# Down product of an expert slot: the last 48 inner rows as two split float32r passes instead of one fp32 product

## The reference

```python
E, K, I, SI = (16, 4, 176, 704)
topk_w, topk_idx = jax.lax.top_k(routing_probs, K)      # 4 of 16 experts per token
shared = _silu_mul(x @ shared_gate_up.T, SI) @ shared_down.T
def step(acc, ew):
    w_gu, w_d, cw = ew
    h = _silu_mul(x @ w_gu.T, I)                        # silu(gate) * up, 176 inner rows
    return (acc + h @ w_d.T * cw[:, None], None)
```

## Time and profile before

| | before |
|---|---|
| median of 3 runs | 1028.64 us (1028.04 to 1030.07) |
| profiled execution, device time | 1030.14 us |
| its span, first to last instruction | 1028.1 us |
| TensorE busy | 962.3 us (94%) |
| VectorE busy | 825.4 us (80%) |
| ScalarE busy | 379.4 us (37%) |
| GpSimd busy | 509.6 us (50%) |
| mean granted TensorE clock | 0.975 |

### The profile page before, as it was taken

How to read it: one execution, slowest core, us unless ns; L and a number is a source line. 1 busy time by engine, 2 the same in 40 slices (tenths; PEclk the granted TensorE clock), 3 DMA queues, 4 the chain that set the end, 5 groups by cost and what they waited for, 6 DMA issues and landing times.

```text
span 1028.1 us, 17347 instructions
## 1 busy us (share of the span) xinstructions
PE 962.3 (94%) x5569; PEld 853.8 (83%) x5569; DVE 825.4 (80%) x1583; ACT 379.4 (37%) x1063; POOL 509.6 (50%) x384
## 2 busy tenths in 40 slices
PE   4799799999999898999999999979899999999997
PEld 4688689888988897888888898867788799999986
DVE  4989989999989999878989988865677766666647
ACT  2454443542333443322345222242154244444430
POOL 0525335366534436575624557614633366666660
PEclk9899999999999999999999999998999999999999
DMA  9789669997347412102521220225151277777769
GB/s 350 281 310 391 260 249 353 408 361 246 144 149 253 187 64 83 62 32 94 207 81 62 83 84 22 75 82 219 53 196 43 80 117 121 120 118 122 118 94 311
DMA packets 67192, 171.84 MB, mean 167 GB/s; under 512 B 6561, under 2 KB 40097, under 8 KB 65953
## 3 DMA queue, kind: packets, MB, share of 16 engines
q1 hardware_dynamic: 52656, 151.69, 40.3%
q0 software_dynamic: 14448, 19.05, 11.3%
HBM read 84.72 MB, written 85.99 MB: 166 GB/s over the span
## 4 chain that ended last, share of the span: by engine, by line
PE 64%; DVE 24%; issue 5%; DMA 3%; POOL 2%; ACT 1%; SPq 0%; DVEq 0%; ACTq 0%; POOLq 0%
PE bank L477 8%; PE bank L479 8%; PE bank L478 8%; DVE rot L1350 5%; PE bank L557 5%; PE bank L687 4%; DVE rot L1347 4%; PE bank L710 4%; PE bank L831 3%; PE bank L833 3%; DVE turn L1334 2%; PE bank L580 2%; PE bank L792 2%; PE bank L582 2%; PE bank L581 2%
## 5 line engine op out<-in xcount | busy, mean ns | idle before, releaser
L1160 POOL TENSOR_TENSOR rot<-turn 64x512 f32<-64x512 f32 x64 | 91.5, 1430 | 260.2 <-DVE turn L1334 234.2
L1334 DVE SCALAR_TENSOR_TENSOR turn<-bank,bqk,trig 128x1024 f32<-128x1024 f32 x128 | 160.7, 1276 | 14.1 <-PE bank L479 12.0
L1228 POOL DMA_INDIRECT sums<-ysb,token_at x79 | 123.0, 1557 | 70.2 <-DMA sums<-ysb,token_at 29.6
L477 PE MATMUL bank<-xt_hi,w_hi 128*128 128x512 f32 x256 | 106.7, 417 | 15.1 <-DVE turn L1334 9.8
L1193 POOL TENSOR_TENSOR kv<-c_t,v_t 128x512 f32<-128x512 f32 x64 | 69.2, 1095 | 98.4 <-ACT v_t L960 46.0
L687 PE MATMUL bank<-wo,z_t 128*128 128x256 f32 x512 | 116.0, 379 | 0.8 <-ACT z_t L1031 0.8
L687 PEld LDWEIGHTS bank<-wo,z_t 128*128 128x128 f32 x512 | 94.9, 190 | 12.8 <-ACT z_t L1031 1.0
L992 ACT ACTIVATE prob<-prob,negmax 128x128 f32<-128x128 f32 x256 | 98.9, 390 | 6.9 <-DVE negmax L1319 6.7
L479 PE MATMUL bank<-xt_hi,w_lo 128*128 128x512 f32 x256 | 100.5, 393 | 0.0
L478 PE MATMUL bank<-xt_lo,w_hi 128*128 128x512 f32 x256 | 100.4, 392 | 0.0
L1002 ACT COPY v<-bank 128x512 f32<-128x512 f32 x64 | 37.5, 586 | 164.2 <-PE bank L479 164.2
(11 more groups left out here) (183 smaller groups left out, 2417.9 us busy)
## 6 DMA issues: line engine op xcount, KB each, us to landing
xs<-zeros SPq DMA_DIRECT2D x12, 3710.0 KB, 16.8
w_hi<-w_dram SPq DMA_DIRECT2D x24, 768.0 KB, 4.4
w_lo<-w_dram SPq DMA_DIRECT2D x24, 768.0 KB, 7.0
xe_all<-xs SPq DMA_DIRECT2D x79, 132.5 KB, 2.6
sums<-zeros SPq DMA_DIRECT2D x3, 2176.0 KB, 12.8
raw<-in_wqkv SPq DMA_DIRECT2D x16, 384.0 KB, 4.3
w_dram<-w_hi SPq DMA_DIRECT2D x8, 768.0 KB, 5.7
w_dram<-w_lo SPq DMA_DIRECT2D x8, 768.0 KB, 7.0
```

The costliest lines, as they stand in the source:

```text
L477: nc.tensor.matmul(o, lh, rh, start=(i == 0), stop=False)
L1228: nc.gpsimd.indirect_dma_start(sums_dram[s % SUMS], bass.IndirectOffsetOnAxis(ap=token_at[:, s:s + 1], axis=0), ysb[s % YBUFS][:], None, c ...
L1334: last = nc.vector.scalar_tensor_tensor(turn_all[m][:, 2 * i:2 * i + 2, :], qk_bank[2 * m + i][:].unsqueeze(1).to_broadcast([128, 2, GT]), ...
```

## The change

The inner rows 128 to 175 no longer go through an fp32 product. `slot_mult` writes them twice into `eh`, at columns 128 to 175 and 192 to 239 (the second by an instruction of its own), so that after the transpose they stand on partitions 0 to 47 and again on 64 to 111. ScalarE takes the turned half as float32r into `rest_hi`; VectorE writes the low part of the upper copy into `rest_lo`, whose lower half is zero. The down weights of these rows, `dnp`, hold their low part on partitions 0 to 63 and their high part on 64 to 127. One pass `rest_hi` x `dnp` then gives high x low plus high x high, and one pass `rest_lo` x `dnp` gives low x high. The low and high parts of `dnp` are made in four parts during the third shared group: ScalarE rounds (two copies of 64x1024, the lower one into the buffer `again`), VectorE subtracts, each waiting for the other. ScalarE's gate goes to a buffer of its own (`sg`) and no longer into `eh`. YBUFS goes from 4 to 3, for room.

```diff
-YBUFS = 4
+YBUFS = 3
...
+PARTS_DOWN = EXPERTS // GB
...
-        eht = [sb(f"eht{i}", [128, 2, 128], c=gctx) for i in range(2)]
+        eht = [sb(f"eht{i}", [128, 128], c=gctx) for i in range(2)]
+        rest_hi = [sb(f"rest_hi{i}", [128, 128], F32R, gctx) for i in range(2)]
+        rest_lo = [sb(f"rest_lo{i}", [128, 128], F32R, gctx) for i in range(2)]
...
-            for part in range(2):
-                e = slice(part * EXPERTS // 2, (part + 1) * EXPERTS // 2)
-                sp.dma_start(dne[:, e], down_in[:, e]).then_inc(down_loaded, 16)
+            sp.dma_start(dnp[:].bitcast(F32), down2_in).then_inc(down_loaded, 16)
+            sp.dma_start(dne[:], down_in).then_inc(down_loaded, 16)
...
                 if s >= 2:
                     pe.wait_ge(eht_taken, s - 1)
+                    pe.wait_ge(rest_lo_done, s - 1)
...
-                nc.tensor.matmul(o, eht[s % 2][:, 0, :], dne[:, e, 0, :].rearrange("p a n -> p (a n)"),
-                                 start=True, stop=False)
-                nc.tensor.matmul(o, eht[s % 2][:, 1, :], dne[:, e, 1, :].rearrange("p a n -> p (a n)"),
-                                 start=False, stop=True).then_inc(ey_ready, 1)
+                w1 = dne[:, e, :].rearrange("p a n -> p (a n)")
+                w2 = dnp[:, e, :].rearrange("p a n -> p (a n)")
+                nc.tensor.matmul(o, eht[s % 2][:], w1, start=True, stop=False)
+                pe.wait_ge(rest_hi_done, s + 1)
+                nc.tensor.matmul(o, rest_hi[s % 2][:], w2, start=False, stop=False)
+                pe.wait_ge(rest_lo_done, s + 1)
+                nc.tensor.matmul(o, rest_lo[s % 2][:], w2, start=False, stop=True).then_inc(ey_ready, 1)
...
+            def rest_high(part):
+                e = slice(part * GB, (part + 1) * GB)
+                if part == 0:
+                    act.wait_ge(down_loaded, 3 * 16)
+                    act.wait_ge(tt_ready, CH * len(TURNS))
+                act.wait_ge(dnp_lo_done, part)
+                nc.scalar.copy(again[0:64].bitcast(F32R), dnp[0:64, e].bitcast(F32))
+                nc.scalar.copy(dnp[64:128, e], dnp[64:128, e].bitcast(F32)).then_inc(dnp_hi_done, 1)
+
             for i in range(SCH):
                 shared_silu(2, i)
+                if i < PARTS_DOWN:
+                    rest_high(i)
+            act.wait_ge(dnp_lo_done, PARTS_DOWN)
...
-                if s >= 2:
-                    act.wait_ge(eht_ready, s - 1)
-                nc.scalar.activation(eh[s % 2][:, 0:INTER], banks[2 + s % 2][:, 0:INTER], ACT.Silu).then_inc(es_done, 1)
+                if s < 2:
+                    act.wait_ge(hm_done, 3 * SCH)
+                else:
+                    act.wait_ge(eh_done, s - 1)
+                nc.scalar.activation(sg[(s + 1) % 2][:, 0:INTER], banks[2 + s % 2][:, 0:INTER], ACT.Silu).then_inc(es_done, 1)
...
-                nc.scalar.copy(eht[s % 2][:], banks[4 + s % 2][:, 0:256].rearrange("p (c t) -> p c t", c=2)).then_inc(eht_taken, 1)
+                nc.scalar.copy(rest_hi[s % 2][:], banks[4 + s % 2][:, 128:256]).then_inc(rest_hi_done, 1)
+                nc.scalar.copy(eht[s % 2][:], banks[4 + s % 2][:, 0:128]).then_inc(eht_taken, 1)
...
+            def rest_low(part):
+                e = slice(part * GB, (part + 1) * GB)
+                dve.wait_ge(dnp_hi_done, part + 1)
+                nc.vector.tensor_tensor(dnp[0:64, e], dnp[0:64, e].bitcast(F32), again[0:64], ALU.subtract).then_inc(dnp_lo_done, 1)
...
+                if i < PARTS_DOWN:
+                    rest_low(i)
...
-                h = eh[s % 2][:, 0:INTER]
-                nc.vector.tensor_tensor(h, banks[2 + s % 2][:, INTER:2 * INTER], h, ALU.mult).then_inc(eh_done, 1)
+                if s >= 2:
+                    dve.wait_ge(eht_ready, s - 1)
+                h, up = sg[(s + 1) % 2][:, 0:INTER], banks[2 + s % 2][:, INTER:2 * INTER]
+                nc.vector.tensor_tensor(eh[s % 2][:, 0:INTER], up, h, ALU.mult)
+                nc.vector.tensor_tensor(eh[s % 2][:, 192:192 + IREST], up[:, 128:INTER], h[:, 128:INTER], ALU.mult).then_inc(eh_done, 1)
...
+            def slot_rest(s):
+                dve.wait_ge(eht_taken, s + 1)
+                if s >= 2:
+                    dve.wait_ge(ey_ready, s - 1)
+                nc.vector.tensor_tensor(rest_lo[s % 2][64:128, :], banks[4 + s % 2][64:128, 128:256],
+                                        rest_hi[s % 2][64:128, :].bitcast(F32), ALU.subtract).then_inc(rest_lo_done, 1)
...
                 if s >= 2:
                     slot_out(s - 2)
+                if 1 <= s <= SLOTS:
+                    slot_rest(s - 1)
```

More of the change, by code:

```diff
@@ L68, in decoder @@
 def decoder(nc, x_in, wqkv_in, bqk_in, bv_in, wo_in, bo_in, trig_in, mask_in, ident_in,
-            ctx_in, ctxt_in, skip_in, toep_in, same_in, gate_in, gue_in, gus_in, down_in, downs_in,
+            ctx_in, ctxt_in, skip_in, toep_in, same_in, gate_in, gue_in, gus_in, down_in, down2_in, downs_in,
             count_in, route_in, out):
@@ L224, in decoder @@
         gue_hi = sb("gue_hi", [128, EXPERTS, CH, 2 * INTER], F32R, ectx)
-        dne = sb("dne", [128, EXPERTS, 2, D], c=ectx)
+        dne = sb("dne", [128, EXPERTS, D], c=ectx)
+        dnp = sb("dnp", [128, EXPERTS, D], F32R, ectx)
         ectx.close()
@@ L331, in decoder @@
         eht_taken = sem("eht_taken")
+        rest_hi_done = sem("rest_hi_done")
+        rest_lo_done = sem("rest_lo_done")
+        dnp_hi_done = sem("dnp_hi_done")
+        dnp_lo_done = sem("dnp_lo_done")
         ey_ready = sem("ey_ready")
@@ L758, in shared_up @@
                     pe.wait_ge(eht_taken, SLOTS - 1)
+                    pe.wait_ge(rest_lo_done, SLOTS - 1)
                     shared_block(SCH - 1 + i, banks[4 + at], q).then_inc(upb_ready, 1)
@@ L775, in shared_up @@
                     pe.wait_ge(eht_taken, SLOTS)
+                    pe.wait_ge(rest_lo_done, SLOTS)
                 if i < SCH - 1 and ups:
@@ L912, in _ @@
             pe.wait_ge(down_loaded, 3 * 16)
+            pe.wait_ge(dnp_hi_done, PARTS_DOWN)
+            pe.wait_ge(dnp_lo_done, PARTS_DOWN)
             experts = [slot_expert(0), None, None, None]
@@ L1718, in _ @@
             for i in range(2):
-                nc.vector.memset(eh[i][:, INTER:256], 0.0)
+                nc.vector.memset(eh[i][:, INTER:192], 0.0)
+                nc.vector.memset(eh[i][:, 192 + IREST:256], 0.0)
+                nc.vector.memset(rest_lo[i][0:64, :].bitcast(F32), 0.0)
             shared_add(2)
@@ L1750 @@
 _INS = ["x", "wqkv", "bqk", "bv", "wo", "bo", "trig", "mask", "ident", "ctx", "ctxt", "skip", "toep", "same", "gate",
-        "gue", "gus", "down", "downs", "count", "route"]
+        "gue", "gus", "down", "down2", "downs", "count", "route"]
 def layouts(x, fside_S2_0, ctx_2048, L0_attn_W_Q, L0_attn_b_Q, L0_attn_W_K, L0_attn_b_K, L0_attn_W_V, L0_attn_b_V,
@@ L1771, in layouts @@
     dwn = a(L0_ffn_expert_down).transpose(2, 0, 1)
-    down = np.zeros((128, EXPERTS, 2, D), np.float32)
-    down[:, :, 0], down[:IREST, :, 1] = dwn[:128], dwn[128:]
+    down2 = np.zeros((128, EXPERTS, D), np.float32)
+    down2[:IREST], down2[64:64 + IREST] = dwn[128:], dwn[128:]
     sdn = a(L0_ffn_shared_down).T
@@ L1801, in layouts @@
         "gus": gus.reshape(SBLK * 128, CH, 128).transpose(2, 1, 0),
-        "down": down,
+        "down": dwn[:128],
+        "down2": down2,
         "downs": downs,
```

## The result

The changed kernel took 1023.97 us (median of 5 runs, 1022.51 to 1024.83), the kernel before, on the same chip, 1030.07 (5 runs, 1028.04 to 1031.82). The ratio is 0.994, 95% interval 0.9921 to 0.9958: a gain of 6.1 us where 15 were forecast, and 1024 lies outside the range of 1011.5 to 1021.5. The profiled execution has a span of 1022.0 us at 1023.97; the span of before was 1028.1, 6.1 more.

The account below looks back on a forecast made before the run. TensorE was taken to bound the slot stage. The profiled 1030.14 us, less 15.1 in the slots, plus 0.3 ahead of them, gave 1015.3, and 1013.8 as median; the 8-in-10 range was 1011.5 to 1021.5.

Parts of the forecast that it names:

- TensorE per slot: Slot stage: two 0.12 us passes replace a 0.434 us fp32 product, period 2.26 to 2.07, saving 0.194 us per slot.
- the 15.1: Forecast TensorE gain over the slots in us: 0.194 x 78, slot 77 left out.
- The ring: Three output buffers in the slots: costs nothing or a few tenths once; rival that it binds, 1035 us, chance 0.03.
- VectorE per slot: Slot stage: two added instructions of 0.14 and 0.29 us stay hidden; idle falls from 0.65 to 0.16 us per slot.
- The thinnest cover: Slots: VectorE's low part is ready 0.25 us before the last pass's weight load; each 0.1 above costs up to 7.9 us.
- ScalarE per slot: Slot stage: one 0.37 us copy becomes two of 0.27, ending 0.07 us later, hidden with 0.4 to spare.
- Before the slots: Splitting the packed down weights ahead of the slots: ScalarE copies and VectorE subtractions cost 0.3 us, bounds 0 and 1.5.
- The first slot transpose should stand at 813.4 as now: Sign in the profile after: TensorE's first transpose of slot rows starts at 813.4 us, unmoved.
- The forecast's last 1.5: Step from the profiled execution's 1015.3 us to the median forecast of 1013.8, as before's profiled execution was 1.5 above its median.
- a cover of 1.64 us: TensorE's 1.64 us idle before the first slot transpose, waiting for a DMA, was to cover the late second block.
- the 1.1 of the prediction: Ahead of the slots: VectorE's L1525 of the second block comes 1.1 us late, and TensorE with it.

Follow-up runs that it names:

- the four buffers: Changed kernel with a fourth ysb buffer (YBUFS = 4) in an idle half of hs; 1021.44 us, ratio 0.9838 to the kernel before.
- the first filler: Changed kernel plus twelve 128x256 products on TensorE ahead of the first slot transpose; 1020.83 us, ratio 0.9844 to the kernel before.
- rows in PSUM: Changed kernel with rounded lower rows in PSUM, a fourth output buffer and twelve products ahead of the first slot transpose; 1020.34 us, ratio 0.9891.
- the padded one: Kernel before plus forty more long-met waits on ScalarE, at about 750 us; 1032.18 us, ratio 1.0017.

## Why the prediction was wrong

- **TensorE per slot: right.** Passes 0.12, period 2.26 to 2.07. Over the 78 periods from first to last turn the medians, 2.260 and 2.073, give 14.6 of the 15.1. The step to 12.9 is slots over the usual period: 2.7 us of them after, 1.0 before. After, two of them (2.42 and 2.29) stand at the full ring and some ten, of 2.1 to 2.3, are scattered. The ring explains 0.3 to 0.6; the others are not settled.
- **VectorE per slot: right.** 0.12 and 0.29 for the forecast 0.14 and 0.29, idle 0.21 for 0.16. The thinnest cover held but for one wait of 0.3.
- **ScalarE per slot: right.** 0.27 each.
- **The ring: right**, a few tenths.
- **Before the slots: wrong, and most of the miss.** The term was "I take 0.3 us in all; bounds are 0 and 1.5", and the sign "The first slot transpose should stand at 813.4 as now". It was 7.0, and the transpose stood at 818.32. From the forecast of 1015.3 for the profiled execution to its 1023.97 there are 8.7 us: 6.7 are this term, 2.2 the slots, -0.2 what follows them. (The forecast's last 1.5, down to the median, fell away: the profiled execution of after is its median.) Without this term's 6.7 the time would have been 1017.3, inside the range. I priced the four subtractions by VectorE's own idle time and took the wait of TensorE for a DMA as a cover of 1.64 us. What was priced came true: TensorE was done with the blocks 26.3 us after the first scatter before and 27.4 after, 1.0 later for the 1.1 of the prediction, and 1.64 would have covered it. What the subtractions did to the thing that TensorE waits for was not in the sum. It was in the trace: three of before's scatters, 1.42, 2.60 and 1.48 us where the others take 0.97, each beside gue_lo. After has 4.4 us more of it. On the chip of 1030, with the splitting left out, the kernel took 1016.61, a ratio of 0.9861 where the forecast is 0.9856, and what is left over before's 33.1 us from first scatter to first turn is 1.8, at a granted clock of 0.79 in 816 to 824. The range had no term for it at all.
- **The clock: missed.** TensorE's idle time rose from 1.64 to 4.81 us, and the fall to 1.2 GHz added 2.1 us (from the first transpose to the first turn 7.4 in place of 5.3). It was not priced. That it follows wholly from the stretched scatters isn't shown: the kernel without splitting, its scatters as before's and its idle time at 1.59, took 7.0 for the same way, and so did before with the forty waits (1.79).

The Trainium skill (SBUF — State Buffer, "SBUF: two separate sides") says that GpSimd and VectorE share one pair of ports, that whoever has it keeps it for the whole instruction, and that an operation of VectorE with both inputs in SBUF holds it against a GpSimd operation that reads SBUF. The traces agree in kind: the same subtraction doesn't stretch a scatter when one operand is in PSUM (0.97 against 1.91 us at 797.8). A single instruction's length doesn't account for all of it: the 5.53 us scatter outlived four such instructions before the one that ended at 807.90. That a scatter counts as an operation that reads SBUF is my reading; no run here shows what part of it waits. I had not applied the rule to the scatters, which I had read as DMAs.

Open is the hold-up of ScalarE (and after it VectorE) for 4 to 16 us at the silu of block 2. No run shows its cause. Eight of the ten profiles from chips of 1037 show a wait of over 4 us released by "remote" there, and none of the ten taken where before took 1028 to 1031. It comes with kernels of either kind; before itself was never profiled on such a chip, so that it loses its 7 us there is a guess. The two changed kernels whose splitting stayed in SBUF in blocks 0 to 3 (the four buffers, and the first filler) had at most 1.6 us of it, and stood at 0.984 of before. The changed kernel itself has no run there, so what the change is worth on such a chip was not measured.

## What to carry to other kernels

In these traces, work put on VectorE while GpSimd issued scatters was not free when both operands were in SBUF, even where VectorE was idle. Look at the lengths of GpSimd's indirect transfers first, and if some are over the usual one, find which VectorE instruction stands beside them. An operand in PSUM took the stretch away (0.97 us beside it), and moving the work two blocks later gave 2.4 us. Moving it to where GpSimd is at rest is the next thing to try; no run here did. And when an engine waits for a DMA, follow that wait back to the engine that issues it before calling the time a cover.

## What the hardware showed unexpectedly

- A scatter that takes 0.97 us undisturbed ended 0.84 to 0.85 us behind the end of a 128x704 subtraction of SBUF operands in each of these cases: 801.87 to 802.72 and 804.93 to 805.77 (before), 800.79 to 801.64, 807.90 to 808.75 and 811.30 to 812.15 (after), 805.16 to 806.01 (rows in PSUM). It isn't always so: the one from 797.81 in after ended 1.12 us behind a 64x1024 subtraction. The longest scatter was 6.63 us, in the kernel before with the four subtractions.
- Idle times of 1.44 to 1.64 us ahead of the first transpose left TensorE's granted clock at 1.00 in the following 8 us in three profiles of before; 1.79 in the padded one went with 0.79, 1.59 in the one without splitting with 0.79 too, and 4.81 in after with 0.57 (over 816 to 824). So the idle time alone doesn't decide it.
- The kernel before takes 1030 us on one chip and 1037 on others, and ScalarE stood still for up to 15.6 us with nothing in the trace that released it, ahead of the same instruction in eight of ten profiles on the latter.
